# Two LSTM recurrences on TensorE: where four matmuls of the output gates stand in a step

## What is computed

```python
def _lstm(x, Wih, Whh, b):
    xW = jnp.einsum('bsd,gd->sbg', x, Wih) + b
    h0 = jnp.zeros((x.shape[0], Whh.shape[1]), x.dtype)

    def step(carry, xt):
        h, c = carry
        gates = xt + h @ Whh.T
        i, f, g, o = jnp.split(gates, 4, axis=-1)
        c = jax.nn.sigmoid(f) * c + jax.nn.sigmoid(i) * jnp.tanh(g)
        h = jax.nn.sigmoid(o) * jnp.tanh(c)
        return ((h, c), h)
    _, hs = jax.lax.scan(step, (h0, h0), xW)
    return jnp.swapaxes(hs, 0, 1)
...
hq = _lstm(hidden_states, Wih_q, Whh_q, b_q)
hk = _lstm(hidden_states, Wih_k, Whh_k, b_k)
```

## Time and profile before

| | us |
|---|---|
| three timed runs | 2268.49, 2268.53, 2270.11; median 2268.53 |
| the profiled execution, its own time | 2268.6 |
| its span, first to last instruction | 2266.8 |
| span of the recurrences' 112 time steps | 65.0 to 384.4 |
| PE busy over the span | 2013.3 (89%) |

### The profile page before, as it was taken

One profiled execution on the slowest core, in us unless ns is written; L12 is line 12 of the kernel. 1 busy time (PEld: TensorE's weight loads), 2 busy tenths in 40 slices (PEclk: granted clock), 3 DMA queues, 4 the chain that ended last, 5 costly groups with the idle time before them and its releaser, 6 DMA issues.

```text
span 2266.8 us, 57634 instructions
## 1 busy us (share of the span) xinstructions
PE 2013.3 (89%) x22720; PEld 1463.7 (65%) x22720; DVE 1339.4 (59%) x3551; ACT 905.5 (40%) x3432; POOL 562.2 (25%) x1360
## 2 busy tenths in 40 slices
PE   8999999999988898998978888998999999789844
PEld 4899998877566565567866655665644545556623
DVE  6677666765355787445645614886263220678787
ACT  2455554443146565202334523665211111346522
POOL 3566665222011000102345512331000000411111
PEclk9555555999999899899998988999999999889965
DMA  3000001004000001200020000000030000000000
GB/s 139 4 5 5 5 5 66 16 1 185 1 5 5 12 12 53 87 0 24 1 100 37 2 1 8 9 12 1 1 154 0 1 0 0 5 11 12 5 0 16
DMA packets 8026, 57.21 MB, mean 25 GB/s; under 512 B 793, under 2 KB 5249, under 8 KB 5985
## 3 DMA queue, kind: packets, MB, share of 16 engines
q1 hardware_dynamic: 7760, 53.54, 6.2%
HBM read 52.62 MB, written 0.92 MB: 24 GB/s over the span
## 4 chain that ended last, share of the span: by engine, by line
PE 68%; DVE 15%; ACT 7%; issue 6%; POOL 4%; DMA 1%; POOLq 0%; DVEq 0%; SPq 0%; ACTq 0%
PE banks L269 43%; PE banks L274 8%; PE banks L1390 6%; PE banks L963 3%; ACT memory L1011 2%; PE banks L989 2%; DVE memory L1492 2%; PE banks L1543 1%; ACT memory L1417 1%; POOL memory L1449 1%; ACT memory L1424 1%; DVE memory L2835 1%; DVE memory L1498 1%; DVE memory L1273 1%; ACT memory L1256 1%
## 5 line engine op out<-in xcount | busy, mean ns | idle before, releaser
L269 PE MATMUL banks<-memory 128*112 128x256 f32 (+8 forms) x4192 | 1126.1, 424 | 99.2 <-DVE memory L3540 21.8
L269 PEld LDWEIGHTS banks<-memory 128*128 128x128 f32 (+3 forms) x4192 | 699.3, 194 | 434.2 <-issue 279.8
L274 PE MATMUL banks<-memory 112*125 112x112 f32 (+3 forms) x2000 | 301.5, 283 | 75.4 <-DVE memory L850 25.7
L274 PEld LDWEIGHTS banks<-memory 112*125 112x125 f32 (+3 forms) x2000 | 234.7, 170 | 190.9 <-issue 99.5
L1390 PE MATMUL banks<-memory 128*128 128x8 bf16 (+2 forms) x10752 | 306.9, 174 | 14.1 <-DVE memory L1475 1.4
L1390 PEld LDWEIGHTS banks<-memory 128*128 128x128 bf16 x10752 | 295.8, 104 | 25.8 <-POOL memory L1449 23.6
L1011 ACT ACTIVATE memory<-banks,memory 112x375 f32<-112x375 f32 x384 | 215.5, 579 | 26.1 <-DVE memory L1049 26.0
L1049 DVE TENSOR_REDUCE memory<-banks 112x2 f32<-112x750 f32 x192 | 171.1, 934 | 39.2 <-PE banks L963 39.0
L1492 DVE TENSOR_REDUCE memory<-banks 128x48 f32<-128x192 f32 x448 | 122.0, 291 | 61.9 <-PE banks L1390 47.6
L1057 DVE COPY memory<-banks 125x448 f32<-125x448 f32 x192 | 117.0, 620 | 9.5 <-PE banks L274 5.1
L1571 ACT ACTIVATE memory<-memory 112x112 f32<-112x112 f32 x192 | 71.7, 374 | 89.0 <-DVE memory L1592 89.0
(11 more groups left out here) (240 smaller groups left out, 2471.8 us busy)
## 6 DMA issues: line engine op xcount, KB each, us to landing
memory<-in_l2x SPq DMA_DIRECT2D x1, 7680.0 KB, 21.5
memory<-in_l2f SPq DMA_DIRECT2D x1, 7168.0 KB, 20.0
memory<-in_l1f SPq DMA_DIRECT2D x1, 4617.0 KB, 14.5
memory<-in_ctxT SPq DMA_DIRECT2D x24, 187.5 KB
memory<-in_l2f SPq DMA_DIRECT2D x1, 4096.0 KB, 12.9
memory<-in_l3f SPq DMA_DIRECT2D x1, 3073.0 KB, 22.3
memory<-in_l2a SPq DMA_DIRECT2D x1, 3072.0 KB, 18.4
memory<-in_l0f SPq DMA_DIRECT2D x1, 2304.0 KB, 9.2
```

The source lines that it names most:

```text
L269: ins = self.nc.tensor.matmul(out, weights[i], acts[i], start=i == 0, stop=i == n - 1)
L274: return self.nc.tensor.transpose(out, in_, self.ident[0:n, 0:n])
```

## The change

```diff
         for t in range(S):
             for l in range(2):
                 for part in (2, 1, 0):
+                    if part == 0:
+                        self.pe_gates(l, 2, 6, GT)
                     if part == 2:
                         PE.wait_ge(*s.h_hi(max(2 * t + l, 1)))
                     elif part == 1 and t:
                         PE.wait_ge(*s.h_mid(2 * t + l - 1))
                     elif part == 0 and t:
                         PE.wait_ge(*s.h_parts(2 * t + l - 1))
                     ins = self.pe_gates(l, part, 0, 6)
                 ins.then_inc(*s.gates_full.up())
-                for part in (2, 1, 0):
+                for part in (1, 0):
                     ins = self.pe_gates(l, part, 6, GT)
                 ins.then_inc(*s.gates_full.up())
```

## The result

The changed kernel takes 2279.38 us in the median (2275.68 to 2282.42, 5 runs) against 2268.53 (2267.68 to 2270.11, 5 runs): ratio 1.0047, 95% interval [1.0033, 1.0060]. It is slower, by 10.9 us; 2280.6 was forecast. The profiled execution took 2280.42 us.

A forecast was written before the change was run, and what follows sets the result against it. One LSTM step's latency was taken to bound the recurrent stage, not PE. Four matmuls at 107 ns a turn over 112 turns add 12.0 us to 2268.6, other terms 0, giving 2280.6 us; range 2276.5 to 2286.5.

The forecast's parts named there:

- What bounds the stage: In the 112 time steps, one LSTM step's latency sets the 2.85 us turn; PE has 0.29 us to spare.
- The price: Four more matmuls ahead of DVE's first sum, 26.7 ns each, add 107 ns to each turn.
- Twelve us in all: Over all 112 time steps, 0.107 us each makes 12.0 us more.
- Low part of h 0.06 us early: Ahead of the step's 25th matmul, h's low part arrives 0.06 us before PE wants it, so no idle to fill.
- The lower bound of the range: At the wait for h's low part, 0.03 us of the four might be covered: 8.6 us, 2277.2 us.
- the upper: Two more switches between PSUM areas per step might cost 26.7 ns each: 18 us, 2286.5 us.
- The output path and PE's work at 0: Output gates' sum starts no sooner, their path has 0.25 us slack; PE keeps 96 matmuls per turn: both worth 0.
- already waited for: Rival: PE stands still at least 107 ns ahead of part 0, which the four fill: no change, 2268.6 us; chance 0.03.
- PE the bound: Rival: PE sets the turn, the four fill its h_parts stalls: 24 us faster, 2244.6 us; chance 0.03.
- Uncovered loads: Rival: the four weight loads lose their overlap, 104 ns each: 46.6 us, 2315.2 us; chance 0.05.
- The clock: Rival: clock rises to 2.4 GHz, spacing 25.0 ns as at the stage's start: +4.5 us, 2273.1 us; chance 0.02.
- the waits: PE's some 111 waits for h grow from 0.21 to about 0.32 us each; DVE's before the first sum by as much.

The follow-up runs named there:

- late_before: Kernel before the change, with POOL's copy of h for later stages put ahead of its writing of h's low part: 2274.70 us.
- interleave: Changed kernel with the four moved matmuls spread one by one among part 0's first eight, still 40 ahead of the first signal: 2282.07 us.
- one_signal: Kernel before the change, with both signals made one behind the step's 48th matmul: 2306.11 us.
- drop_out4: Kernel before the change, without the four matmuls of the output gates' lowest weight part, behind the first signal: 2266.15 us.
- later_before: Kernel before the change, with POOL's copy of h made twice ahead of its writing of h's low part: 2309.74 us.
- later_after: Changed kernel with POOL's copy of h made twice ahead of its writing of h's low part: 2311.71 us.
- drop_other4: Kernel before the change, without four other-gate matmuls (blocks 4 and 5, lowest weight part) ahead of the first signal: 2265.82 us.

## Why the prediction was right, point by point

- What bounds the stage: shown. Twelve us for every four matmuls ahead of the signal, three times over, and none for eight fewer in a turn behind it.
- The price, 26.7 ns a matmul and 107 ns a turn: measured 2.96 against 2.85 us, x40 in 1.26 us against x36 in 1.15. By the load's record of 104 ns, or by the rule of the section "LDWEIGHTS (loading the stationary operand)" of the Trainium skill's page "TensorE: Matmul & The Clock Gate", it would have been about four times that; the runs agree with the spacing of the starts. For the fast load the prediction took four chunks at once as four times the speed. The section "Weight-path perf modes — Fast Weight Load (FWL) and DoubleRow" of that page of the Trainium skill has fourfold as the theory for fp8 and about twofold as measured, by which the four would cost some 213 ns, an estimate. Measured are 107.
- Twelve us in all: stage +12.0. In the profiled executions the rest of the program makes +11.8 of it (1.0 more ahead, 1.2 less behind); that the 10.9 us of the medians come about in the same way isn't shown. That the median lies 1.2 us from the 2280.6 is in part luck: the changed kernel's second set has 2283.8.
- Low part of h 0.06 us early, so nothing to fill: shown by late_before, where 0.11 us of delay made 0.05 us of stall. The lower bound of the range, with some of the four covered, didn't come true; nor did the upper, since interleave gave switches no price.
- The output path and PE's work at 0: shown by one_signal (three times the price with the output sum no earlier) and drop_out4.
- The rivals: already waited for needs a low part that comes later than it does, and is what later_before and later_after are. PE the bound: refuted by drop_out4. Uncovered loads: 96 loads in 2.64 us. The clock: the granted clock was 0.50, its 1.2 GHz level, from 69.2 us to the stage's end, and it rose nowhere in between.
- Off in a detail: the waits. DVE's, forecast to grow by as much as PE's, 11.4 us, grew by 12.1 in all (in the list of waits by 20.4, as more of them are long enough to be in it). For PE's loads I forecast some 111 waits of 0.32 us, 35 us in all. There were 112, of 28.0 us, for in 64 turns the idle was split between the two LSTMs' steps. The turn was as long there, so nothing hung on it. What parts the two after five turns and joins them again I can't say.

No version faster than the kernel before came out of this: drop_other4, the one with a shorter chain, leaves out work and still gains only 2.9 us of stage.

## What to carry to other kernels

In a recurrence, count the instructions ahead of the signal that the chain waits for, not how busy the engine is: PE was 96% busy, and yet taking 8 of 96 matmuls away gained nothing, while moving the same 8 ahead of the signals cost 12.0 us of the stage. Before work is put ahead of a wait to fill it, look whether the engine stands still there: a stream of evenly spaced starts says no, however plausible the wait looks in the code. And a margin of 0.06 us is one that the next edit uses up: whoever shortens such a chain must look at every wait on it, the middle ones too.

## What was not expected of the hardware

An instruction put between two dependent ones on POOL cost far less than its length: the copy of 0.27 us delayed the low part by 0.11 us. Some 0.08 us of it lay in a gap that POOL had left there before, and the rest of what was hidden is overlap with its neighbours in the records. A second copy, which itself had to wait for the first, brought the stall from 0.05 to 0.33 + 0.08 = 0.41 us (part 0 at 1.05 us in place of 0.64). And the program behind the stage, the same in all these kernels, took from 1875.1 to 1888.0 us in single executions: more than the whole effect of the change.
